# A graph network's one-hot aggregation: loops of five tiles for three, window ranges packed in one number, partial sums and keys moved to GpSimd

## Chip, cores and metric

The kernel runs on one core of a Trainium2 chip. The metric is the device time of one execution in microseconds. The engines are TensorE (PE, with its weight loads shown as PEld), VectorE (DVE), ScalarE (ACT), GpSimd (POOL) and SyncE (SP); each has a sequencer (shown as PEq or PEldq, DVEq and so on) that reads its own stream of instructions, register and branch instructions among them.

## The reference

The whole program is two layers of a network over 625 nodes with 512 features and 20000 edges sorted by `dst`. The change touches its first stage alone, which computes from the layer-normed features `xn`:

```python
hp = xn @ weight                                   # 625 x 512
msgs = hp[src] * edge_weight[:, None]
agg = relu(segment_sum(msgs, dst, num_segments=625))
```

and the counts of edges between each pair of nodes, which later attention layers use as a mask. `src` is uniform over the nodes; `dst` is `625 * u**2` for uniform u, sorted, so that low nodes have many edges. Behind it follow linear attention, a mixture of experts, two attention layers over the graph and a second mixture.

## The kernel before

**Tiles and windows.** The 20000 edges lie as 160 tiles (ET) of 125 edges, one edge on each partition. The nodes as destinations are cut into 20 windows (NW) of 32 (DW). For each window the kernel multiplies, over all tiles that hold an edge of it, a one-hot matrix of the edge's source (`one_src`, 125 edges x 628 columns) by a matrix of its destination (`hot_dst`, 125 x 128: the one-hot of the 32 destinations times the three bf16 parts of the weight, and once more by 1 for the count). Five matmuls of 128 columns, one for each 125 sources, make a tile. They add up in PSUM, in two banks a window, so that four windows have room.

**Start.** SyncE loads src, dst and the weights, then the features in one DMA, the product weights `gnnW` and `mixWq` beside it (lines 301 to 307). DVE works out windows, keys (1024 x window + source) and weight parts (lines 1111 to 1126), the first and the last tile of each window by PE's turning and two scans (1143 to 1151), the one-hot of the destinations for all tiles (`dst_one`, line 1139, ahead of the scans) and, behind the layer norm (1089 to 1105), its products with the three weight parts (1158, `dst_parts`). PE turns the numbers of the ranges into a row (543), DVE copies it to `bounds` (1153), PE turns the normalized rows (502) and multiplies them by gnnW (514, stage `hp`, 40 matmuls and as many weight loads), and ACT takes both out (913, 919). GpSimd zeroes two DRAM buffers by 35 DMAs (431, 434).

**The window loop.** PE and DVE run the same loops with k read at run time, three tiles (GT) a trip. DVE (line 1183) waits until PE has freed one of the GT buffers of `one_src`, then compares 628 numbers with `key - 1024 * w`, in one instruction of two operations. PE (line 581) waits for it and multiplies. Two matmuls by zero open a window's banks (569) and two close them (586). ACT copies the counts out (932); DVE adds the three weight parts (1170) one window later. Each window's first tile, its trips and the trips before it are three register loads from `bounds`, on PE (552 to 554) and on DVE (1162 to 1164). Both engines issue them one window ahead in program order, which puts them at the end of the window before. The loop's register steps are lines 575 and 1178.

**Behind it.** PE goes on with `mq` (526), whose banks wait for the sums, then turns the counts (599) and multiplies the summed weights by hp (605).

## Time and profile before

| | us |
|---|---|
| median of three runs | 1304.54 (1303.4 to 1308.75) |
| the profiled execution | 1310.6, its span 1309.1 |
| PE busy | 1117.8 (85%) |
| DVE busy | 540.6 (41%) |
| ACT busy | 347.6 (27%) |
| POOL busy | 83.4 (6%) |
| L581, PE, 975 matmuls | 85.6 busy, 44.5 idle before them |
| L1183, DVE, 195 comparisons | 66.9 busy, 63.3 idle before them |

A busy PE counts matmuls from start to modelled end, so neighbours overlap: 15 of 219 ns each may take 1.01 us in all. The stretches of the busy view give, for each engine, busy us and in brackets the number of instructions, in the order PE, PEld, DVE, ACT, POOL; then the clock granted to TensorE as a share of 2.4 GHz, the DMA engines' busy share, and GB/s. In the timeline the brackets at a row's end hold the idle time before it and what ended it; "issue" is nothing that the profile shows. Register instructions do not count as busy; the view by line and the chain of waits show them.

### The profile page before, as it was taken

To read this page: it belongs to the slowest core of one execution; us is meant where nothing else is said; L and a number is where in the kernel's file an instruction comes from. 1 tells how busy PE (TensorE), PEld (TensorE's weight loads), DVE (VectorE), ACT (ScalarE), POOL (GpSimd) and SP (SyncE) were. 2 spreads that over 40 slices of the span, in tenths; PEclk is the share of its full clock that TensorE was granted. 3 is DMA by queue.
4 is the path that set the end of the run, shared out by engine and by line. 5 is a ranking of instruction groups with operands and counts; after the bars stand their busy time and mean duration, and the time that the engine had idled before them with its cause. 6 is when DMAs were issued, how large, how long until landed. Compare 5 with 4: busy or idle time off the path is not lost.

```text
span 1309.1 us, 19993 instructions
## 1 busy us (share of the span) xinstructions
PE 1117.8 (85%) x7185; PEld 757.1 (58%) x7186; DVE 540.6 (41%) x1434; ACT 347.6 (27%) x881; POOL 83.4 (6%) x130
## 2 busy tenths in 40 slices
PE   2766679988999863999998659998979998988896
PEld 1456564465877651555554347777557777565652
DVE  7565565343555431111111035444325544376430
ACT  1000012012555430222222125554115555011320
POOL 5100000000000032001000050000000000000000
PEclk9897789998999975999999969999989999998898
DMA  7500004010100046940199671000111000000000
GB/s 198 141 1 1 1 1 193 32 57 17 31 26 3 1 185 244 388 177 19 60 401 398 244 271 43 25 9 2 64 73 41 25 9 2 33 1 0 1 1 39
DMA packets 18415, 113.06 MB, mean 86 GB/s; under 512 B 4718, under 2 KB 6245, under 8 KB 14135
## 3 DMA queue, kind: packets, MB, share of 16 engines
q1 hardware_dynamic: 12718, 100.95, 20.3%
q0 software_dynamic: 5632, 11.23, 3.3%
q8 instruction: 43, 0.70, 0.2%
q14 instruction: 22, 0.18, 0.0%
HBM read 103.04 MB, written 9.11 MB: 86 GB/s over the span
## 4 chain that ended last, share of the span: by engine, by line
PE 74%; DVE 8%; DMA 7%; issue 4%; ACT 3%; DVEq 3%; POOL 1%; SPq 0%; POOLq 0%; ACTq 0%
PE psum L514 11%; PE psum L669 8%; PE psum L819 7%; PE psum L800 7%; PE psum L692 5%; PE psum L526 5%; PE psum L723 5%; PE psum L674 4%; PE psum L705 4%; PE psum L581 4%; PE psum L878 3%; PE psum L900 3%; DMA arena<-in_moe_b 2%; PE psum L502 1%; DVE arena L1183 1%
## 5 line engine op out<-in xcount | busy, mean ns | idle before, releaser
L514 PE MATMUL psum<-arena 128*125 128x512 f32 x320 | 142.2, 605 | 2.6 <-ACT arena L913 2.0
L581 PE MATMUL psum<-arena 125*128 x975 | 85.6, 260 | 44.5 <-DVE arena L1183 41.4
L971 ACT ACTIVATE arena<-arena,small 125x625 f32<-125x625 f32 x120 | 97.0, 809 | 90.5 <-DVE small L1312 90.5
L669 PE MATMUL psum<-arena 128*128 128x313 f32 (+1 forms) x384 | 112.2, 443 | 8.5 <-DMA arena<-in_att 7.2
L800 PE MATMUL psum<-arena 128*64 128x512 f32 x448 | 101.7, 607 | 7.4 <-DMA arena<-in_moeW 6.0
L514 PEld LDWEIGHTS psum<-arena 128*125 128x125 f32 x320 | 60.9, 192 | 80.7 <-issue 74.9
L581 PEld LDWEIGHTS psum<-arena 125*128 125x128 bf16 x975 | 74.2, 119 | 54.5 <-issue 52.2
L819 PE MATMUL psum<-arena 128*64 128x256 f32 x896 | 99.8, 381 | 3.7 <-DMA arena<-in_moe_b 3.7
L1029 ACT ACTIVATE arena<-psum,cols 128x64 f32<-128x64 f32 x224 | 47.3, 361 | 198.6 <-PE psum L806 198.6
L669 PEld LDWEIGHTS psum<-arena 128*128 128x128 f32 x384 | 72.2, 194 | 37.9 <-issue 9.7
L1183 DVE TENSOR_SCALAR arena<-arena 125x628 bf16<-125x628 f16 x195 | 66.9, 382 | 63.3 <-issue 28.0
L1312 DVE CUSTOM_DVE_ANT_0 arena<-psum,cnt_adj 125x625 f32<-125x625 f32 x80 | 61.5, 807 | 71.8 <-PE psum L692 71.8
L723 PE MATMUL psum<-arena 125*64 125x125 f32 x1200 | 77.4, 274 | 9.5 <-ACT arena L983 9.0
L819 PEld LDWEIGHTS psum<-arena 128*64 128x64 f32 x896 | 63.4, 137 | 36.2 <-ACT arena L1029 5.8
L979 ACT ACTIVATE arena<-psum 125x500 f32<-125x500 f32 x120 | 63.7, 583 | 74.7 <-PE psum L705 74.7
L692 PE MATMUL psum<-arena 64*125 64x113 f32 x480 | 80.3, 453 | 0.0
L723 PEld LDWEIGHTS psum<-arena 125*64 125x64 f32 x1200 | 63.2, 136 | 25.1 <-ACT arena L983 12.3
L800 PEld LDWEIGHTS psum<-arena 128*64 128x64 f32 x448 | 32.6, 140 | 68.8 <-issue 66.8
L526 PE MATMUL psum<-arena 128*128 128x312 f32 (+1 forms) x256 | 68.3, 427 | 0.8 <-DVE arena L1332 0.8
L705 PE MATMUL psum<-ident,arena 125*125 125x125 f32 x480 | 67.8, 284 | 0.0
L692 PEld LDWEIGHTS psum<-arena 64*125 64x125 f32 x480 | 52.5, 183 | 24.9 <-issue 16.1
L502 PE MATMUL psum<-ident,arena 125*128 125x125 f32 x140 | 27.1, 366 | 44.4 <-DVE arena L1105 37.4
(242 smaller groups left out, 1335.6 us busy)
## 6 DMA issues: line engine op xcount, KB each, us to landing
arena<-in_moeW SPq DMA_DIRECT2D x16, 4096.0 KB, 17.7
arena<-in_att SPq DMA_DIRECT2D x36, 256.0 KB, 2.8
arena<-in_l1W SPq DMA_DIRECT2D x2, 2048.0 KB, 15.7
rows<-in_rows SPq DMA_DIRECT2D x1, 2500.0 KB
token_rows<-arena POOLq DMA_DIRECT2D x19, 128.0 KB, 10.5
expert_rows<-arena POOLq DMA_DIRECT2D x17, 128.0 KB, 10.0
arena<-token_rows POOLq DMA_DIRECT2D x16, 128.0 KB, 8.3
arena<-in_gnnWo SPq DMA_DIRECT2D x2, 1024.0 KB, 6.2
```

Of the source, the lines that this page charges most:

```text
L514: mm = pe.matmul(bank(b, NP, D), srcT[:, k, c * NP:(c + 1) * NP], ring[n % 2][:, k, :], start=(k == 0), stop=(k == KC - 1))
L526: mm = pe.matmul(bank(b, P, w), ring[n % 2][:, k, m * P:(m + 1) * P], srcT[:, k, o:o + w], start=(k == 0), stop=(k == KC - 1))
L581: mm = pe.matmul(psum[:, o + c * P:o + (c + 1) * P], one_src[:, s, c * NP:c * NP + P], hot_dst[:, bass.ds(e * P, P)], start=False, stop=False,
L669: mm = pe.matmul(bank(b, P, width), aw[:, w, k, :], srcT[:, k, o:o + width], start=(k == 0), stop=(k == KC - 1))
L692: mm = pe.matmul(psum[0:NP, at_:at_ + n], q[h * HD:(h + 1) * HD, c * NP:(c + 1) * NP], k[h * HD:(h + 1) * HD, o:o + n], start=True, stop=True)
L705: mm = pe.transpose(bank(3 + h, NP, NP, NP * j), Sx[u % 3][h][:, j * NP:(j + 1) * NP], ident[0:NP, 0:NP])
L723: mm = pe.matmul(psum[h * HD:(h + 1) * HD, 5 * 512 + 256:5 * 512 + 256 + NP], vv[i % 2][:, j, h * HD:(h + 1) * HD], PT[:, u % 2 * NC + j, ...
L800: mm = pe.matmul(psum[q * TT:(q + 1) * TT, 512 * b:512 * b + D], xsT[:, k4, :], EW1[par][:, k4, o:o + D], start=(k4 == 0), stop=(k4 == KC ...
L819: mm = pe.matmul(psum[q * TT:(q + 1) * TT, 4 * 512:4 * 512 + D // 2], hT[:, f, :], EW2[par][:, f, q * (D // 2):(q + 1) * (D // 2)], start= ...
L971: act.activation(Sx[u % 3][h], Sx[u % 3][h], ACT.Exp, bias=small[0:NP, 80 + n:81 + n], scale=-1.0, accum_out=small[0:NP, 120 + n:121 + n]) ...
L979: act.activation(PT[:, u % 2 * NC:u % 2 * NC + 4, h * NP:(h + 1) * NP], bank(3 + h, NP, 4 * NP).rearrange("p (j n) -> p j n", j=4), ACT.Co ...
L1183: ve.tensor_scalar(one_src[:, s, :], iota_src[:, 0:SW], float(1024 * w), key[:, bass.ds(e, 1)], ALU.add, ALU.is_equal).then_inc(hot_ready, 1)
```

## The change

- `GT` is 5 for 3: five buffers of `one_src`, five tiles a trip.
- `bounds` holds one number a window, 64 x first tile + trips. PE and DVE each read all twenty into registers ahead of the loops, take the parts by shift and mask (`tile_range`), and keep the sum of trips in a register. PE's reads stand behind hp.
- DVE compares in one operation, with keys that GpSimd has made for the window (`key_w`, two buffers, made a window ahead).
- ACT copies the counts and then the three weight parts of each window to SBUF (`parts`), GpSimd adds them by two instructions. PE's bank waits are for ACT's copy. The sums have to be there ahead of `agg`.
- The features come in five DMAs ahead of all product weights; gnnW is asked for once they are in, mixWq and the rest once gnnW is. GpSimd's zeroing waits for gnnW.
- `dst_one` moves from ahead of the range arithmetic to behind the layer norm; the statistics of each chunk of features move ahead of the copy of `bounds`.

```diff
@@ -26,11 +26,12 @@
...
 ET = EDGES // NP
-GT = 3
+GT = 5
+KG = -(-ET // GT)
 TP = ET + GT - 1
...
 NW = -(-N // DW)
-SW = N + GT
+SW = N + 3
 EX = 8
@@ -175,14 +176,17 @@
...
 zero_bf = take(NP, P, dt=BF16)
-zero_rows_sb = take(TT, D)
+zero_rows_sb = at(o_D + TP * 2 * DW, TT, D)
 t_lo, t_hi = take(ET // 2, 2), take(ET // 2, 2)
...
 w_end = take(NW, 8)
-w_cols = take(NW, 3)
+w_cols = take(NW, 2)
 n_i = take(NW, 2, dt=I32)
-bounds = take(1, 3, WMIN, dt=I32)
+bounds = take(1, WMIN, dt=I32)
+key_w = [take(NP, TP) for i in range(2)]
+parts = [at(o_T + 2 * KC * N + i * NC * 3 * DW, NP, NC, 3 * DW) for i in range(2)]
+assert o_D + TP * 2 * DW + D <= AR
 assert oa[0] <= o_cnt
@@ -238,7 +242,8 @@
...
 unit_full, freed_a, freed_v = sem("unit_full"), sem("freed_a"), sem("freed_v")
-ld_edges, ld_x, ld_const = sem("ld_edges"), sem("ld_x"), sem("ld_const")
+ld_edges, ld_const = sem("ld_edges"), sem("ld_const")
+ld_x = [sem(f"ld_x{c}") for c in range(NC)]
 ld_ring = [sem(f"ld_ring{i}") for i in range(2)]
...
@@ -296,16 +303,22 @@
...
+def tile_range(eng, packed):
+    return (eng.snap(packed >> 6, min_val=0, max_val=ET - 1), eng.snap(packed & 63, min_val=1, max_val=KG))
+
 @block.sync
...
     sp.dma_start(wgt, ins["edge_w"]).then_inc(ld_edges, 16)
-    sp.dma_start(xres[:], ins["x"]).then_inc(ld_x, 16)
+    for c in range(NC):
+        sp.dma_start(xres[:, c, :], ins["x"][:, c, :]).then_inc(ld_x[c], 16)
+    for c in range(NC):
+        sp.wait_ge(ld_x[c], 16)
     sp.dma_start(ring[0], ins["gnnW"]).then_inc(ld_ring[0], 16)
+    sp.wait_ge(ld_ring[0], 16)
     sp.dma_start(ring[1], ins["mixWq"]).then_inc(ld_ring[1], 16)
     sp.dma_start(cols[:], ins["cols"]).then_inc(ld_const, 16)
-    sp.wait_ge(ld_x, 16)
     sp.dma_start(rows[:], ins["rows"].partition_broadcast(NP)).then_inc(ld_const, 16)
@@ -424,7 +437,7 @@
...
-    pool.wait_ge(ld_x, 16)
+    pool.wait_ge(ld_ring[0], 16)
     pool.wait_ge(consts, 14)
@@ -433,7 +446,22 @@
...
-    pool.wait_ge(win_full, NW)
+    def window_keys(w):
+        pool.tensor_scalar(key_w[w % 2], key, float(-1024 * w), None, ALU.add).then_inc(keys_out, 1)
+
+    pool.wait_ge(key_ready, 1)
+    window_keys(0)
+    window_keys(1)
+    for w in range(NW):
+        pool.wait_ge(parts_out, w + 1)
+        if w + 2 < NW:
+            window_keys(w + 2)
+        n = min(DW, N - DW * w)
+        p3 = parts[w % 2].rearrange("p c (v d) -> p c v d", v=3)
+        pool.tensor_tensor(p3[:, :, 0, 0:n], p3[:, :, 0, 0:n], p3[:, :, 1, 0:n], ALU.add).then_inc(part_sum, 1)
+        pool.wait_ge(part_sum, w + 1)
+        pool.tensor_tensor(WT[:, :, DW * w:DW * w + n], p3[:, :, 0, 0:n], p3[:, :, 2, 0:n],
+                           ALU.add).then_inc(wt_out, 1)
     pool.memset(bd[:, :, :], 0.0).then_inc(bd_zero, 1)
@@ -539,19 +567,15 @@
...
     pe.wait_ge(range_cols, 1)
-    for v, spread in enumerate((ident, ident, upper)):
-        mm = pe.matmul(bank(5, 1, WMIN, WMIN * v), w_cols[:, min(v, 1):min(v, 1) + 1], spread[0:NW, 0:WMIN],
-                       start=True, stop=True)
-    mm.then_inc(range_rows, 1)
-    pe.wait_ge(range_ready, 1)
+    pe.matmul(bank(5, 1, WMIN), w_cols[:, 1:2], ident[0:NW, 0:WMIN],
+              start=True, stop=True).then_inc(range_rows, 1)
     rows_to_cols("xnT0", N1, lambda c: pe.wait_ge(ln_out, c + 1))
...
-    def tile_range(w):
-        return (pe.value_load(bounds[0:1, 0, w:w + 1], min_val=0, max_val=ET - 1),
-                pe.value_load(bounds[0:1, 1, w:w + 1], min_val=1, max_val=-(-ET // GT)),
-                pe.value_load(bounds[0:1, 2, w:w + 1], min_val=0, max_val=NW * -(-ET // GT)))
+    pe.wait_ge(range_ready, 1)
+    ranges = [pe.value_load(bounds[0:1, w:w + 1], min_val=1, max_val=64 * ET + KG) for w in range(NW)]
+    before = 0
@@ -559,19 +583,16 @@
...
     stage_out(pe, "hp")
-    ahead = tile_range(0)
     for w in range(NW):
-        first, k, before = ahead
+        first, k = tile_range(pe, ranges[w])
         o = window_banks(w)
         if w >= 4:
-            pe.wait_ge(wt_out, w - 3)
+            pe.wait_ge(parts_out, w - 3)
         for q in range(2):
...
             mm.then_inc(hot_free, GT)
-        if w + 1 < NW:
-            ahead = tile_range(w + 1)
         with pe.Fori(0, k) as j:
@@ -586,12 +607,14 @@
...
         mm.then_inc(win_full, 1)
+        before = pe.snap(before + k, min_val=w + 1, max_val=(w + 1) * KG)
...
         w = NW - 4 + (unit % 8) // 2
-        pe.wait_ge(wt_out, w + 1)
+        pe.wait_ge(parts_out, w + 1)
     product_cols("mq", T1, 1, window_out)
+    pe.wait_ge(cnt_out, NW)
     for c in range(NC):
@@ -599,6 +622,7 @@
...
         mm.then_inc(unit_full, 2)
+    pe.wait_ge(wt_out, NW)
     for c in range(NC):
@@ -929,9 +953,11 @@
...
         o, n = 512 * (2 * (w % 4)), min(DW, N - DW * w)
-        act.activation(cntT[:, :, DW * w:DW * w + n],
-                       psum[0:NP, o:o + NC * P].rearrange("p (c v d) -> p c v d", v=4, d=DW)[:, :, 3, 0:n],
-                       ACT.Copy).then_inc(cnt_out, 1)
+        sums = psum[0:NP, o:o + NC * P].rearrange("p (c x) -> p c x", x=P)
+        act.activation(cntT[:, :, DW * w:DW * w + n], sums[:, :, 3 * DW:3 * DW + n], ACT.Copy).then_inc(cnt_out, 1)
+        if w >= 2:
+            act.wait_ge(wt_out, w - 1)
+        act.activation(parts[w % 2], sums[:, :, 0:3 * DW], ACT.Copy).then_inc(parts_out, 1)
@@ -1119,7 +1145,7 @@
...
     ve.tensor_copy(w_part[:, 0, 0:ET], w_hi)
-    ve.scalar_tensor_tensor(key[:, 0:ET], win, 1024.0, srcf, ALU.mult, ALU.add)
+    ve.scalar_tensor_tensor(key[:, 0:ET], win, 1024.0, srcf, ALU.mult, ALU.add).then_inc(key_ready, 1)
     link(ve.tensor_tensor(w_rest, wgt, w_hi, ALU.subtract))
@@ -1136,8 +1162,6 @@
...
     i_.then_inc(range_in, 1)
-    ve.tensor_tensor(hot_dst4[:, :, 3, :], low.unsqueeze(2).to_broadcast([NP, TP, DW]),
-                     iota_dst.unsqueeze(1).to_broadcast([NP, TP, DW]), ALU.is_equal).then_inc(dst_one, 1)
     ve.wait_ge(range_turned, 1)
@@ -1148,43 +1172,36 @@
...
     link(ve.tensor_scalar(n_i[:, 1:2], n_i[:, 0:1], 16, None, ALU.logical_shift_right))
-    ve.tensor_copy(w_cols[:, 1:2], n_i[:, 1:2]).then_inc(range_cols, 1)
+    ve.scalar_tensor_tensor(w_cols[:, 1:2], w_cols[:, 0:1], 64.0, n_i[:, 1:2], ALU.mult,
+                            ALU.add).then_inc(range_cols, 1)
+    for c in range(NC):
+        ve.wait_ge(ld_x[c], 16)
+        i_ = chunk_stats(xres, c)
+    link(i_)
     ve.wait_ge(range_rows, 1)
-    ve.tensor_copy(bounds, bank(5, 1, 3 * WMIN).rearrange("p (v w) -> p v w", v=3)).then_inc(range_ready, 1)
-    ve.wait_ge(ld_x, 16)
-    layer_norm(0, xres, N1)
+    ve.tensor_copy(bounds, bank(5, 1, WMIN)).then_inc(range_ready, 1)
+    layer_norm(0, xres, N1, stats=False)
+    ve.tensor_tensor(hot_dst4[:, :, 3, :], low.unsqueeze(2).to_broadcast([NP, TP, DW]),
+                     iota_dst.unsqueeze(1).to_broadcast([NP, TP, DW]), ALU.is_equal).then_inc(dst_one, 1)
     ve.wait_ge(dst_one, 1)
...
-    def tile_range(w):
-        return (ve.value_load(bounds[0:1, 0, w:w + 1], min_val=0, max_val=ET - 1),
-                ve.value_load(bounds[0:1, 1, w:w + 1], min_val=1, max_val=-(-ET // GT)),
-                ve.value_load(bounds[0:1, 2, w:w + 1], min_val=0, max_val=NW * -(-ET // GT)))
-
-    def window_sums(w):
-        ve.wait_ge(cnt_out, w + 1)
-        o, n = 512 * (2 * (w % 4)), min(DW, N - DW * w)
-        parts = psum[0:NP, o:o + NC * P].rearrange("p (c v d) -> p c d v", v=4, d=DW)
-        ve.tensor_reduce(WT[:, :, DW * w:DW * w + n], parts[:, :, 0:n, 0:3], AX, ALU.add).then_inc(wt_out, 1)
-
     ve.wait_ge(range_ready, 1)
-    ahead = tile_range(0)
+    ranges = [ve.value_load(bounds[0:1, w:w + 1], min_val=1, max_val=64 * ET + KG) for w in range(NW)]
+    before = 0
     for w in range(NW):
-        first, k, before = ahead
-        if w + 1 < NW:
-            ahead = tile_range(w + 1)
+        first, k = tile_range(ve, ranges[w])
+        ve.wait_ge(keys_out, w + 1)
         with ve.Fori(0, k) as j:
...
                 ve.wait_ge(hot_free, (before + j) * GT + s + 1)
-                ve.tensor_scalar(one_src[:, s, :], iota_src[:, 0:SW], float(1024 * w), key[:, bass.ds(e, 1)],
-                                 ALU.add, ALU.is_equal).then_inc(hot_ready, 1)
-        if w:
-            window_sums(w - 1)
-    window_sums(NW - 1)
+                ve.tensor_scalar(one_src[:, s, :], iota_src[:, 0:SW], key_w[w % 2][:, bass.ds(e, 1)], None,
+                                 ALU.is_equal).then_inc(hot_ready, 1)
+        before = ve.snap(before + k, min_val=w + 1, max_val=(w + 1) * KG)
```

## Rows read from the trace of the kernel before

**Rows 1.** Busy time of each engine by stretch (columns: see the profile section).

```profile
53.40:60.00 6.60, 6.42 (x64) 6.04 (x65) 4.30 (x12) 0.00 (x0) 0.00 (x0) 0.57 0.25 55
60.00:90.00 30.00, 20.71 (x312) 17.10 (x308) 19.71 (x60) 0.64 (x3) 0.00 (x0) 1.00 0.01 2
90.00:183.50 93.50, 61.22 (x680) 55.35 (x681) 52.57 (x140) 5.17 (x17) 0.00 (x0) 0.73 0.00 1
```

**Rows 2.** Timeline, merged: start us, us, engine line operation, count, [idle before <-releaser].

```profile
61.10 1.05 PE L581 MATMUL psum<-arena 125*128 x15 [0.27 <-DVE arena L1183]
...
61.80 0.97 DVE L1183 TENSOR_SCALAR arena<-arena 125x628 bf16<-125x628 f16 x3 [0.35 <-PE psum L581]
...
100.12 4.35 PE L581 MATMUL psum<-arena 125*128 x42 [2.11 <-DVE arena L1183]
...
102.68 1.35 DVE L1183 TENSOR_SCALAR arena<-arena 125x628 bf16<-125x628 f16 x3 [0.25 <-PE psum L581]
```

**Rows 3.** Chain of waits at a boundary between windows: start us, us, what.

```profile
124.74 0.31 DVEq L1163
...
125.37 0.30 DVEq L1164
```

**Rows 4.** PE's queue by line: count, ns min/median/max, first to last start us.

```profile
L552 PEldq TENSOR_LOAD <-arena x2: 522/614/707, 47.5 to 50.4; - x2
...
L552 PEldq TENSOR_LOAD <-arena x18: 297/302/310, 71.2 to 177.5; - x18
...
L552 PEldq FUSED_REGOPS  x18: 168/168/168, 71.6 to 177.8; - x18
...
L581 PEldq FUSED_REGOPS  x3: 69/69/153, 73.6 to 74.1; - x3
...
L575 PEldq ALU_OP  x1: 32/32/32, 74.3 to 74.3; - x1
...
L575 PEldq FUSED_REGOPS  x1: 56/56/56, 74.7 to 74.7; - x1
```

**Rows 5.** Timeline, the last window's first matmuls.

```profile
182.64 1.01 PE L581 MATMUL psum<-arena 125*128 x15 [0.31 <-DVE arena L1183]
```

**Rows 6.** Timeline of the start, 14 to 51 us.

```profile
14.81 0.30 DVE L1143 TENSOR_TENSOR arena<-psum,arena 20x160 f32<-20x160 f32 x1
...
17.24 0.14 DVE L1151 CAST arena<-arena 20x1 f32<-20x1 int32 x1
...
19.29 3.07 DVE L1089 BATCH_NORM_STATS2 small<-xres 125x6 f32<-125x512 f32 x5 [0.68 <-DMA xres<-in_x]
...
26.16 16.48 DVE L1158 TENSOR_TENSOR arena<-arena 125x5184 bf16<-125x5184 bf16 x3
...
29.29 17.43 PE L514 MATMUL psum<-arena 128*125 128x512 f32 x40 [0.68 <-ACT arena L913]
...
46.76 0.60 ACT L919 ACTIVATE arena<-psum 125x512 f32<-125x512 f32 x1 [2.84 <-PE psum L514]
...
50.34 0.28 PE L569 MATMUL psum<-arena 125*128 125x64 f16 x2 [3.62 <-issue]
```

**Rows 7.** By line, the expert stage: PE's queue behind 32 matmuls, and these.

```profile
L804 PEldq FUSED_REGOPS  x1: 43/43/43, 567.0 to 567.0; - x1
...
L800 PE MATMUL psum<-arena x32: 592/592/592, 564.4 to 570.9; 128*64 128x512 f32 x32
```

**Rows 8.** DMA issues: what, count, KB each, us to landing.

```profile
arena<-in_mixWp SPq DMA_DIRECT2D x1, 1024.0 KB, 4.9
```

**Rows 9.** By line and in groups: GpSimd operations, and DVE's beside one.

```profile
L442 POOL TENSOR_TENSOR arena<-arena,rows x5: 1257/1260/1648, 470.0 to 475.2; 125x512 f32<-125x512 f32 x5
...
L1105 DVE TENSOR_SCALAR arena<-arena,small x5: 545/546/551, 468.1 to 469.9; 125x512 f32<-125x512 f32 x5
...
L413 POOL IOTA arena<- 20x160 f32 x1 | 0.3, 254 | 0.0
```

**Rows 10.** Groups by shape, DVE at 200 to 206 us: busy us, mean ns.

```profile
L1205 DVE TENSOR_SCALAR cnt_adj<-psum 125x625 f32<-125x625 f32 x2 | 1.6, 800 | 0.0
```

More of the change, by code:

```diff
@@ L252, in build @@
         hot_ready, hot_free = sem("hot_ready"), sem("hot_free")
-        win_full, wt_out, cnt_out = sem("win_full"), sem("wt_out"), sem("cnt_out")
+        win_full, cnt_out = sem("win_full"), sem("cnt_out")
+        key_ready, keys_out = sem("key_ready"), sem("keys_out")
+        parts_out, part_sum, wt_out = sem("parts_out"), sem("part_sum"), sem("wt_out")
         fm_min, fm_exp = sem("fm_min"), sem("fm_exp")
```

## Prediction

> **What bounds it now.** I read the busy time by stretch first. The whole aggregation stage, in which one-hot matrices are built by VectorE and multiplied by TensorE, lies between 53.4 and 183.5 us, 130.1 of the span's 1309.1, and in it no engine is full: look at how PE and DVE both stay near two thirds or below, and at the granted clock, 0.57 and then 1.00 in the first stretches and 0.73, a mix of 1.2 and 2.4 GHz, over the last 93.5 us [rows 1]. Then the timeline inside the stage. At full clock a trip of three tiles repeats every 1.33 us: PE works 1.05 and waits 0.27 for DVE, DVE works 0.97 and waits 0.35 for PE [rows 2]. Neither is slow; with three buffers the round trip through both sets the pace. At 1.2 GHz the trip takes 1.60 (DVE's 1.35 and 0.25 of waiting for PE) and PE goes through without a gap, 42 matmuls in 4.35: there it is PE's own pace, 0.53 a tile [rows 2]. Third, the chain between two windows: DVE's queue spends 0.63 us on each of three register loads (the second begins at 124.74, the third at 125.37), and PE stands idle 2.11 us at such a boundary [rows 2, 3]. PE's own queue has the same loads, 0.30 for the read and 0.15 to 0.17 for the check behind it, about 0.66 each, so it would be no earlier [rows 4]. The one boundary where no load is left costs PE 0.31 us of idle time instead [rows 5]. Fourth, the start: DVE is busy with the one-hot parts until 42.6, PE with hp until 46.7 and ACT until 47.4, then three loads on PE to 50.3, and three more until its first product at 53.4 [rows 1, 6].
>
> Everything behind 183.5 waits for this stage by the chain, and no load with a fixed time falls due there, so what the stage saves moves the end by as much.
>
> **How many tiles.** Counting the reference's inputs, the 20 windows touch 37, 16, 13, 11, 9, 9, 8, 8, 7, 7, 6, 6, 6, 6, 6, 5, 6, 5, 5 and 3 tiles. In threes that is 65 trips and 195 tiles; the trace has 975 = 5 x 195 matmuls there. In fives it is 46 trips (8, 4, 3, 3, then eleven times 2, 1, 2, 1, 1, 1) and 230 tiles: 35 tiles more are multiplied, each 0.28 to 0.30 at full clock (15 matmuls in 1.01 to 1.05 us, 219 ns the last) and 0.53 at half [rows 2, 5].
>
> **Loops of five.** Five buffers lift the round trip: 1.33 us for five tiles would be 0.27 a tile, below what either engine needs. What is left is PE's queue. Its waits for the three tiles start from 73.6 to 74.1, the loop's add and register step, with the branch between them, run at 74.3 and 74.7, and with the next wait's own 0.1 a trip of three can't be under about 1.2 [rows 4]. Two more tiles at 0.24 to 0.28 make 1.7 to 1.8; I take 1.71. DVE starts a comparison every 0.29 (three in 0.97, the last 0.38), so 1.45 a trip and about 1.55 with its branch: just faster [rows 2]. 46 trips x 1.71 = 78.7. In the first 6 us after PE's idle time the clock is 1.2 GHz as it is now [rows 1], where a trip takes 5 x 0.53 = 2.67: two trips more by 0.96, +2.
>
> **Packed ranges.** Twenty times three loads leave both queues' windows. Instead each window has three register steps (shift, mask, running sum). The trace has one of this kind a trip, 56 ns [rows 4], 0.1 with its gap; at most it costs what follows a load, 0.36. I take 0.1, since the loop's own step has bounds too and no check stands behind it: 0.3 a window, 0.3 to 1.1. With the boundary's 0.07 above a trip's own end (from the one boundary without loads [rows 5]) 20 x 0.37 = 7. Sum of the stage: 78.7 + 2 + 7 = 88.
>
> **The loads move to the front, twenty in a row, on each queue.** On DVE they run under the one-hot parts (0.63 x 20 = 12.6 in 22 us) as its first six do now. On PE they stand behind hp. 20 x 0.66 = 13.2, or 17.6 at the 0.88 that the 0.52 to 0.71 us reads of 47 to 54 us gave [rows 4]. How far can PE's queue run ahead of the matmuls? In the expert stage the register step behind 32 matmuls ran at 567.0 while they went on to 570.9, with 18 of the 32 still ahead [rows 7]. Eighteen of hp's 40 at 0.43 (17.43 us for 40 [rows 6]) are 7.7 us.
>
> **The start itself.** dst_one (5.5 us) leaves the gap before the range arithmetic, which so begins 4.7 us earlier, at 10.1 behind PE's turning, and ends at 12.7 instead of 17.4 [rows 6]. The features come alone now: 1.25 MB at the pace of 1 MB in 4.9 us [rows 8] is 6.1 us, with the five issues at 10 to 11 us, so the statistics start at 12.7 and not 19.3, and hp's weights, asked for after them, land near 16 to 17 (bound 22, where they would be used). 6.6 us earlier, less 0.3 for the bounds' copy that now stands behind them: the normalized rows and all of hp move by -6.3, hp from 29.3 to 23.0 and its end from 46.7 to 40.4, ACT's to 41.1 [rows 6]. DVE's four one-hot operations (5248 elements for 5184) run 19.9 to 42.2, as late as now: this edit buys nothing on DVE, 6.3 us on PE. PE's loads then run from 40.4 - 7.7 = 32.7 to 46 or 50; I take 47.4, and with it the opening matmul. From there to the first product lie one comparison and two handovers, which in a trip take 0.35 and 0.62 (61.10 to 61.80 to the next product at 62.43), with 0.2 for the register steps 1.2: 48.6 instead of 53.4, -4.8. Bounds 44.4 (all of them under hp) and 59.6 (none).
> The Trainium skill (Advanced Engine Details and Errata, Engine Queue Depths) gives TensorE's queue as 64 entries; then 64 of hp's 80 loads and matmuls would be queued, PE's registers would be ready by 40 to 44, and DVE's 42.2 would decide: 4 us better. The row above shows no more than 36 entries.
>
> **Sums elsewhere.** DVE loses 20 reductions of 0.65; ACT copies 480 columns (about 0.58, like its 512-column copies of 0.60 [rows 6]) beside 0.31 for the counts: 0.9 a window of at least 2.1, hidden. PE's bank wait goes to the copy, four windows back: nothing. The last sum is needed behind mq, 17 us later: nothing. GpSimd gets a key step and two additions a window. Additions of 512 columns take 1.26, so 160 at most 0.55 each, 160 numbers by one input near an iota's 0.25 and up to 0.35 [rows 9]: 1.45 a window, 29 in all. Keys are made a window ahead: hidden, unless GpSimd falls behind. It might: one of its additions at 470.0 began beside the last two of DVE's five normalizing operations (to 470.5) and took 1.65 for 1.26 [rows 9], so GpSimd waits while such a DVE operation runs. DVE is free for 88 - 230 x 0.29 = 21 us of 88; GpSimd wants 29. Between 0 and 19 (below); I take 5. Keys 0 and 1 stand behind its 35 zeroing DMAs, which started when the features were in, at 19.3, and now start when hp's weights are, near 17: through before the loops as now; were they late, the first product would be so one for one. **The single comparison**: same size and types, one operation less. No row separates the two, so 0, from -0.1 a comparison (hidden behind PE's queue anyway) to the case below.
>
> **Sum.** Stage 93 for 130.1: -37. Start -4.8. Together -42. The profiled execution took 1310.6 with its launch, so 1268.6 in its terms; the median of the runs shown is 6.1 lower, 1304.5, so **1262.5**.
>
> **Rivals.**
> - *PE's twenty loads don't hide.* Against: the run-ahead in [rows 7]. For: they are twice as many as it covers. First product at 59.6, stage as forecast: 1304.5 + 6.2 - 37 = 1274. Chance 0.12.
> - *The clock stays a mix.* Now it falls in the short windows and not in the long ones [rows 1]; PE will be busier in each (a boundary of 0.7 us for 2.1 idle), which speaks against it. If half of the 28 trips from window 4 on are at 1.2 GHz: 14 x 0.96 = +13.4, 1276; all of them 1289. Chance 0.15.
> - *GpSimd and DVE exclude each other.* Each of GpSimd's 1.45 us then also stops DVE: 46 x 1.55 + 20 x 0.33 + 29 = 107 for the stage, 1304.5 - 4.8 - 23 = 1277. DVE's operations beside the slow addition took 551 for 545 ns, so it was GpSimd alone that paid; but they were first. The Trainium skill (SBUF — State Buffer, SBUF: two separate sides) has this as a rule: an exclusive lock for a whole instruction, against a DVE operation in a two-port mode. Chance 0.14.
> - *Slower: the comparison in its new form loses its rate.* The two-operation form does 628 columns in 0.38; other comparisons of DVE take 0.80 for 625 [rows 10]. At 0.72 from start to start 230 of them are 165 us, the stage 172: 1304.5 - 4.8 + 42 = 1342. It decides from about 0.55 a comparison on, where 230 of them equal the time now. Speaking against it: types, sizes and memory are unchanged. Chance 0.05. With it goes a remainder of 0.04 for a start or a register step that costs far more than any row.
> - *The change does little*, since the boundary is waits and not loads: against it stands the one boundary without loads. 1300 to 1306, 0.04.
>
> **Range and chances.** Forecast 0.46 (1250 to 1272). Unknown terms: start -9 to +6, register steps 0 to +16, GpSimd -5 to +14, clock 0 to +27. From 1247 (all at their good ends: start 44.4, stage 86, less a little) to 1292 lie the forecast and the first three rivals. About 0.5%, 6.5 us, is what a measurement can tell from no change: faster by more 0.88, within 0.05, slower 0.07.
>
> **What would show it.** Right: COMPARE_BRANCH of PE's loop 46 times; trips 1.7 apart at full clock with PE idle 0.3 in each; PE idle 0.6 to 0.8 between windows; first product near 48.6 and last near 142; clock 1.00 behind 60 us; DVE comparisons at 0.38. Wrong: TENSOR_LOADs on PE ending behind 52; PE trips of 2.67; DVE comparisons ended by GpSimd's key step, or GpSimd additions above 1 us; checks behind each register step. The forecast fails if PE's queue needs over 2.2 us a trip, or if the clock is at 1.2 GHz for most of the stage.

## Result and the profile after

The changed kernel takes 1322.2 us (median of 4 runs, 1319.0 to 1325.9) where the kernel before took 1304.0 on the same chip: ratio 1.0133, interval 1.0095 to 1.0171. It is 1.3% slower, with an interval clear of 1, where 1262.5 us was forecast, and outside the range.

| | before | after | forecast |
|---|---|---|---|
| profiled execution, us | 1310.6 | 1319.0 | 1268.6 |
| first product of a trip, us | 53.4 | 48.1 | 48.6 |
| last product's start | 183.4 | 199.4 | about 142 |
| stage of windows, us | 130.0 | 151.3 | 93 |
| behind the last product, to the span's end | 1125.7 | 1117.8 | as before |

The start came 5.3 us earlier, as forecast. The stage became 21 us longer instead of 37 shorter. What lies behind it holds the same work; in the profiles of the changed kernel and of the twelve kernels below it took 1118 to 1126 us, so a difference of some us between single profiles can come from there. Stage and first product are each read from one profile too.

Groups of the page (busy us, mean ns of one | idle time before, its releaser): PE's products, their weight loads, VectorE's comparisons.

```profile
L602 PE MATMUL psum<-arena 125*128 x1150 | 86.3, 242 | 63.5 <-issue 43.1
...
L602 PEld LDWEIGHTS psum<-arena 125*128 125x128 bf16 x1150 | 78.5, 110 | 69.7 <-issue 69.6
L1202 DVE TENSOR_SCALAR arena<-arena 125x628 bf16<-125x628 f16 x230 | 77.1, 393 | 75.6 <-PE psum L602 67.0
```

PE stands idle 63.5 us ahead of these products, and 43.1 of it wait for nothing the profile shows ("issue"). DVE's 75.6 us of idle time wait for PE. The comparisons themselves cost 393 ns: nothing wrong there.

Busy time of each engine by stretch of the stage, columns as in [rows 1]:

```profile
48.10:64.00 15.90, 14.76 (x204) 13.87 (x204) 13.30 (x42) 0.00 (x0) 0.00 (x0) 0.83 0.31 75
64.00:100.00 36.00, 23.78 (x396) 21.98 (x395) 25.74 (x75) 4.59 (x12) 9.92 (x18) 1.00 0.00 1
100.00:140.00 40.00, 18.39 (x291) 16.98 (x289) 17.54 (x56) 3.83 (x10) 8.36 (x16) 0.94 0.00 1
140.00:199.80 59.80, 32.25 (x347) 30.31 (x346) 19.84 (x59) 6.12 (x16) 12.69 (x23) 0.64 0.01 2
```

PE's busy share falls from stretch to stretch: 14.76 of 15.90 us, then 23.78 of 36, 18.39 of 40. (In the last stretch it rises to 32.25 of 59.8, because at the lower clock each product takes longer.) The granted clock is a mix of 1.2 and 2.4 GHz in the first stretch (0.83), at its upper level of 2.4 GHz to 100 us, just below (0.94) to 140, and a mix again (0.64) over the last 60 us. So this is not a stage with a bad engine but one that gets worse as it goes. The timeline shows how, first in window 0:

```profile
56.99 1.56 PE L602 MATMUL psum<-arena 125*128 x25 [0.32 <-DVE arena L1202]
...
58.77 1.57 PE L602 MATMUL psum<-arena 125*128 x25 [0.22 <-DVE arena L1202]
59.50 1.56 DVE L1202 TENSOR_SCALAR arena<-arena 125x628 bf16<-125x628 f16 x5 [0.22 <-PE psum L602]
...
60.56 0.56 PE L602 MATMUL psum<-arena 125*128 x7 [0.23 <-DVE arena L1202]
```

From 56.99 to 58.77 a trip of five tiles takes 1.78 us, with PE idle 0.22 to 0.32 for DVE: the trip that was forecast at 1.71. In window 9 the same two rows read:

```profile
118.84 1.56 PE L602 MATMUL psum<-arena 125*128 x25 [1.94 <-issue]
...
119.60 1.56 DVE L1202 TENSOR_SCALAR arena<-arena 125x628 bf16<-125x628 f16 x5 [2.05 <-PE psum L602]
...
122.66 1.05 PE L602 MATMUL psum<-arena 125*128 x16 [2.26 <-issue]
123.41 0.38 DVE L1202 TENSOR_SCALAR arena<-arena 125x628 bf16<-125x628 f16 x1 [2.26 <-PE psum L602]
```

Here a trip takes 3.82 us (118.84 to 122.66). The products still need 1.56, but PE is idle 2.26 ahead of the next trip, and DVE idles just as long behind it. PE's queue in that gap (count, ns min/median/max, first to last start):

```profile
L600 PEldq ALU_OP  x16: 32/39/43, 120.5 to 122.1; - x16
L600 PEldq FUSED_REGOPS  x1: 56/56/56, 122.2 to 122.2; - x1
```

Line 600 is the wait for a tile's comparison. Its value needs `before`, and ahead of one wait PE's queue works through sixteen ALU_OPs, of 0.04 us each and 0.107 from one to the next (120.5 to 122.1 for 16). Over the whole stage, for PE's wait and for DVE's:

```profile
L600 PEldq ALU_OP  x748: 32/36/43, 48.1 to 197.6; - x187
L600 PEldq FUSED_REGOPS  x38: 50/56/56, 64.0 to 196.5; - x38
```
```profile
L1201 DVEq ALU_OP  x745: 40/45/53, 48.2 to 194.0; - x187
L1201 DVEq FUSED_REGOPS  x38: 63/70/77, 62.8 to 192.9; - x38
```

On PE, 184 of them are what the five waits of 46 trips need (one for each tile but the first); the other 564 are the running sum. `before = pe.snap(before + k)` doesn't put a number into a register. `before` stays an expression over the packed ranges of all earlier windows, (r0 & 63) + (r1 & 63) + ..., and it is worked out anew wherever it is used, which is in every trip. Counting a mask and an addition for each earlier window, the 46 trips hold 318 such pairs, 636 steps; the trace has 564 ALU_OPs and one FUSED_REGOPS in each of the 38 trips behind window 0, which must stand for the rest.

So a trip grows by 0.2 us with every window, from 1.78 us to 5.2 and more near the end (from 180.40 to 185.59, with the matmuls by zero that close and open a window in between):

```profile
180.40 2.82 PE L602 MATMUL psum<-arena 125*128 x25 [2.24 <-issue]
...
185.59 2.15 PE L602 MATMUL psum<-arena 125*128 x25 [2.24 <-issue]
```

The products of the trip at 180.40 run at the lower clock, 2.82 us instead of 1.56, and still PE is idle for 2.24 before the next ones: even there it is the queue that sets the trip, not the clock. Two trips of window 12 show it side by side: the one from 142.58 us has its products at 1.2 GHz (2.82 us) and takes 4.51 us, the one from 147.09 has them at 2.4 GHz (1.56 us) and takes 4.43. And it is PE's queue more than DVE's, which works out the same sums: the chain of waits from 100 to 199 us is PE's products for 46.0%, "issue" right ahead of them for 37.7%, DVE's comparisons for 12.4% and DVE's queue for some 4%. No run left the expression on one of the two queues alone.

### The profile page after: what moved, and what is told of

The parts are those of the page before. It is cut to its first block, busy times and chain, and to the rows that moved or that the text cites. A ratio compares the mean times of both kernels' runs of the same rounds, so it can differ in the third digit from the quotient of the medians.

```text
span 1317.2 us, 21595 instructions
## 1 busy us (share of the span) xinstructions
PE 1113.8 (85%) x7356; PEld 755.5 (57%) x7357; DVE 541.5 (41%) x1449; ACT 356.9 (27%) x901; POOL 119.0 (9%) x190
## 4 chain that ended last, share of the span: by engine, by line
PE 75%; DVE 8%; issue 6%; DMA 5%; ACT 3%; DVEq 1%; POOL 1%; SPq 0%; POOLq 0%; ACTq 0%
PE psum L542 9%; PE psum L693 9%; PE psum L843 7%; PE psum L824 6%; PE psum L602 6%; PE psum L716 5%; PE psum L554 5%; PE psum L747 5%; PE psum L698 4%; PE psum L729 4%; PE psum L902 3%; PE psum L924 3%; DMA arena<-in_moe_b 2%; PE psum L629 2%; DVE arena L1202 2%
## 5 line engine op out<-in xcount | busy, mean ns | idle before, releaser
L602 PE MATMUL psum<-arena 125*128 x1150 | 86.3, 242 | 63.5 <-issue 43.1
L602 PEld LDWEIGHTS psum<-arena 125*128 125x128 bf16 x1150 | 78.5, 110 | 69.7 <-issue 69.6
L1202 DVE TENSOR_SCALAR arena<-arena 125x628 bf16<-125x628 f16 x230 | 77.1, 393 | 75.6 <-PE psum L602 67.0
```

The lines of the kernel that those rows point to most:

```text
L602: mm = pe.matmul(psum[:, o + c * P:o + (c + 1) * P], one_src[:, s, c * NP:c * NP + P], hot_dst[:, bass.ds(e * P, P)], start=False, stop=False,
L1202: ve.tensor_scalar(one_src[:, s, :], iota_src[:, 0:SW], key_w[w % 2][:, bass.ds(e, 1)], None, ALU.is_equal).then_inc(hot_ready, 1)
```

## Experiments

Times are medians; ratios are to the kernel before, measured beside each (1306 to 1307 us), and go by all runs, so they need not be the quotient of the medians. First product and stage come from each kernel's one trace. The start is the same in eight of the kernels (total, total3, hoist, two_op, one_input, both, sums_dve, fours), but for GpSimd's first keys, and yet their first products came at 47.9 to 52.0 us: that much single profiles differ there.

| kernel | us | ratio, 95% interval | first product | stage |
|---|---|---|---|---|
| total | 1271.1 | 0.9731 (0.9675, 0.9786) | 48.9 | 97.1 |
| total3 | 1278.2 | 0.9780 (0.9722, 0.9839) | 50.8 | 106.7 |
| lazy_before | 1295.5 | 0.9896 (0.9859, 0.9934) | 53.7 | 120.1 |
| lazy_mask | 1368.1 | 1.0463 (1.0418, 1.0508) | 53.7 | 192.1 |
| start_only | 1301.0 | 0.9957 (0.9936, 0.9977) | 47.4 | 128.8 |
| hoist | 1267.1 | 0.9683 (0.9646, 0.9719) | 51.5 | 93.8 |
| two_op | 1265.9 | 0.9687 (0.9654, 0.9721) | 52.0 | 92.4 |
| one_input | 1271.9 | 0.9737 (0.9704, 0.9771) | 51.2 | 93.0 |
| both | 1264.7 | 0.9670 (0.9648, 0.9691) | 51.9 | 87.3 |
| sums_dve | 1263.2 | 0.9670 (0.9641, 0.9699) | 51.0 | 85.9 |
| fours | 1260.0 | 0.9666 (0.9633, 0.9699) | 47.9 | 90.8 |
| loads_spread | 1262.1 | 0.9666 (0.9647, 0.9684) | 43.2 | 97.6 |

### Is it the expression?

**total** keeps the changed kernel and holds the sum in one register of each queue; the same on DVE's side:

```
-            before = 0
+            total = pe.alloc_register("total_pe")
+            pe.reg_mov(total, 0)
             ...
+                before = pe.snap(total, min_val=w, max_val=w * KG)
             ...
-                before = pe.snap(before + k, min_val=w + 1, max_val=(w + 1) * KG)
+                pe.reg_add(total, total, k)
```

> The changed kernel, with one difference: the running number of trips lives in a register of its own on PE and on DVE, set to 0, read at each window's start, and increased by k once at each window's end, where the changed kernel wrote the sum as an expression that is worked out again in every trip (in the trip at 118.8 us 14 extra ALU_OPs on PE, 2 for each earlier window, about 0.1 us each). Theory (the expression is what fails the prediction): no ALU_OPs that grow with the window, trips of about 1.8 us in all windows at full clock, first product still near 48, last near 140 to 148, so 52 to 60 us less than the changed kernel: 1262 to 1272 us. Rival (GpSimd's key step and additions on the port it shares with DVE): trips still grow or DVE's comparisons still wait, the stage keeps 130 us or more, over 1300 us. Rival (TensorE's clock): the stage is at 1.2 GHz from about 140 us on as it was, 1280 to 1290.

Measured 1271.1 us, 51 less than the changed kernel. PE's waits have no ALU_OP left but a tile's own, and behind 64 us the clock stays at its upper level (PE's wait line, then the stretches):

```profile
L602 PEldq ALU_OP  x184: 32/32/42, 48.9 to 145.2; - x184
```
```profile
48.80:64.00 15.20, 14.02 (x194) 13.21 (x195) 12.68 (x40) 0.00 (x0) 0.00 (x0) 0.83 0.29 73
64.00:100.00 36.00, 29.68 (x463) 26.00 (x460) 30.34 (x87) 5.36 (x14) 11.25 (x21) 1.00 0.00 1
100.00:146.00 46.00, 37.77 (x574) 32.49 (x573) 38.11 (x104) 9.19 (x24) 20.93 (x36) 1.00 0.01 2
```

564 ALU_OPs fewer make the stage 54.2 us shorter, 0.096 us for each, where they lay 0.103 apart on average (0.107 in the gap above): nine tenths of their time had been on the path. And the lower clock of the last 60 us is gone with PE's waiting.

**lazy_before** puts such an expression alone into the kernel before: its third number a window is no longer loaded but summed from the loaded counts.

```
-                        pe.value_load(bounds[0:1, 2, w:w + 1], ...)
+                before = pe.snap(before + k, min_val=w + 1, ...)
```

> The kernel before, with one difference: the third number of each window (trips before it) is not loaded but written as the sum of the trips of all earlier windows, as the changed kernel does. Here each earlier window is one addition (its trips are a loaded register), not a mask and an addition. Theory: each trip of window w gets w more ALU_OPs of about 0.1 us on PE and 0.07 to 0.08 on DVE, 416 in all by the trips (13, 6, 5, 4, six times 3, nine times 2, 1): 42 us of PE's queue, of which one load a window saved (0.66 x 19 = 12.5) and some slack in the trips at 1.2 GHz go off: slower than before by 10 to 30 us. Rival (the expression costs nothing that matters): one load less a window, faster by up to 12 us.

A miss: it got 11 us faster. The trace tells why. The loop's own register line, with up to nineteen terms in it, and the wait's line:

```profile
L575 PEldq FUSED_REGOPS  x65: 50/175/195, 53.4 to 171.8; - x65
L575 PEldq ALU_OP  x65: 32/32/32, 54.2 to 173.5; - x65
```
```profile
L579 PEldq ALU_OP  x140: 32/32/42, 53.7 to 173.2; - x140
L579 PEldq FUSED_REGOPS  x28: 42/128/180, 119.1 to 172.3; - x28
```

A sum of plain registers is put together into one FUSED_REGOPS, 175 ns where [rows 4] shows 56, once a trip, and the wait's line has 140 ALU_OPs in all. In exchange one load of three is gone from each window, and the stage is 9.9 us shorter. So "an expression instead of a loaded value" was not yet the cause; my second guess was that the mask in it is.

**lazy_mask** is lazy_before with `& 63` on each loaded count, which changes no value.

```
-                        pe.value_load(bounds[0:1, 1, w:w + 1], ...)
+                        pe.snap(pe.value_load(bounds[0:1, 1, w:w + 1], ...) & 63, ...)
```

> The kernel before with the sum of earlier trips as an expression (as in lazy_before, 1295.5 us), and each loaded count masked with 63 ahead of the sum, which changes no value. Theory (the mask is what costs: two ALU_OPs for each earlier window in every trip, 0.205 us together in the changed kernel's trace, while a plain addition is folded into the FUSED_REGOPS): 65 trips hold 416 such pairs, 85 us of PE's queue, of which some 20 us hide beside the products: 1360 us, 1335 to 1380. Rival (the length of the sum costs, or the one load less, whatever is summed): as lazy_before, 1290 to 1300.

```profile
L580 PEldq ALU_OP  x864: 32/36/43, 53.7 to 244.6; - x173
L580 PEldq FUSED_REGOPS  x52: 50/56/56, 72.9 to 244.0; - x52
```
```profile
100.00:245.00 145.00, 67.78 (x625) 60.03 (x624) 49.03 (x129) 4.89 (x16) 0.00 (x0) 0.52 0.00 1
```

1368.1 us: 724 ALU_OPs more than lazy_before's 140, a stage 72.0 us longer, 0.099 us for each. It is the same price as between the changed kernel and total, from the other side, and here too the clock falls to a mix (0.52) as PE waits more. The mask keeps the terms from being put together, and the sum then costs about two ALU_OPs a term in every trip (724 for 416 terms). The only difference between the two kernels is the mask on the loaded count, so this settles the cause.

**hoist** is total with `first` and `k`, too, written into registers once a window, three register steps a window as the prediction had them:

```
-            return (eng.snap(packed >> 6, ...), eng.snap(packed & 63, ...))
+            eng.reg_alu(first_r, packed, 6, ALU.logical_shift_right)
+            eng.reg_alu(k_r, packed, 63, ALU.bitwise_and)
+            return (eng.snap(first_r, ...), eng.snap(k_r, ...))
```

> The kernel total (1271.1 us), with first and k also written into registers once a window, so that no shift and no mask is left inside a trip. Theory (PE's queue is part of what sets a trip's length): two ALU_OPs of 0.09 us with their gaps leave each of 46 trips, 0 to 5 us of the time: 1269, 1266 to 1272. Rival (the comparisons of DVE set the trip, at 0.29 us a tile and 0.6 us beside GpSimd): nothing, 1271 within 1.5.

1267.1 us, with a stage of 93.8 us for the 93 of the forecast. Against total the times' intervals overlap; the stage is 3.3 us shorter, within the expected 0 to 5.

### What are the other parts worth?

**start_only** is the kernel before with only the reordered start (chunks of the features ahead of hp's weights, statistics ahead of the one-hot, dst_one behind them).

> The kernel before with the reordered start alone: features in five DMAs ahead of the weights, gnnW behind them, statistics of the chunks ahead of the copy of the bounds, the one-hot of the destinations behind the layer norm, zeroing behind gnnW. Loops, loads, sums and keys as before. Theory: first product of the windows moves from 53.4 to about 48.2 (DVE's one-hot parts end near 42.2, then six loads on PE), everything behind it shifts: 1299 us, 5 less. Rival (the start is hidden by other work or the later transfers fall into the loop): 1304.

1301.0 us, 5 less; as expected. The stage is 128.8 us, as good as before's 130.0.

**total3** is total with `GT = 3`, so 65 trips and 195 tiles.

> As the run with the total in a register, but three tiles a trip and three buffers instead of five (65 trips, 195 tiles). It tells what the fives are worth without the expression. Theory: trips of 1.33 us bound by the round trip through three buffers, boundaries of about 1 us: 65 x 1.33 + 20 x 0.4 = 94 at full clock, some of it at 1.2 GHz (1.60): a stage of 95 to 105, 1270 to 1282 us. If fives are worth much, it is 10 or more above the run with five; if the 35 extra tiles eat the gain, the same within 5.

Fives against threes: a stage of 97.1 for 106.7 us, 7 us in the medians, though the intervals of the two ratios overlap. The expectation had "10 or more" or "within 5" and got neither. Total3 against start_only, which has threes too, tells what the packed ranges are worth, with the sums and keys on GpSimd: a stage of 106.7 for 128.8 us and 1278.2 for 1301.0. That is the largest gain in the change, 22 us of the stage. Part of it comes back by the clock: the granted clock over the stage is 0.78 in start_only and 0.99 in total3. **fours** is the kernel "both" (below) with `GT = 4`: 54 trips, 216 tiles.

> The kernel both with loops of four tiles instead of five: 54 trips and 216 tiles instead of 46 and 230. Theory (14 tiles fewer at 0.31 to 0.37 us, and 8 ends of a trip more at 0.35 to 0.5 us): 1 us less, within 3: 1261 to 1267. Rival (a shorter buffer starves PE: the wait for DVE's first comparison grows with it): 1270 or more, as threes cost 7 us.

1260.0 us is 1 below the expected range. There is no difference to fives in the times (0.9666 and 0.9670), with a stage of 90.8 us for 87.3: the trips added cost the stage 3.5 us more than the tiles saved give, and the times can't tell it.

**two_op** is total with DVE's comparison of before and no key by GpSimd.

```
-                        ve.tensor_scalar(one_src[...], iota_src[...], key_w[w % 2][:, bass.ds(e, 1)], None, ALU.is_equal)
+                        ve.tensor_scalar(one_src[...], iota_src[...], float(1024 * w), key[:, bass.ds(e, 1)], ALU.add, ALU.is_equal)
```

> The kernel total with DVE's comparison of before (add and is_equal from the one key) and without GpSimd's 20 key operations. Theory (both comparisons run at the same rate, 0.382 us in the trace of before and 0.376 in total's; GpSimd's key is free): 1271 within 2. Rival (the single comparison is worth what its place in the change suggests): 1276 or more.

The comparison in both forms (total's with one operation, two_op's with two):

```profile
L1206 DVE TENSOR_SCALAR arena<-arena x230: 369/377/717, 48.2 to 144.9; 125x628 bf16<-125x628 f16 x115
```
```profile
L1197 DVE TENSOR_SCALAR arena<-arena x230: 370/378/680, 51.3 to 143.0; 125x628 bf16<-125x628 f16 x115
```

377 and 378 ns in the median, 382 on average in the kernel before. The single comparison buys nothing, and its keys cost GpSimd 0.64 us a window. The time without them, 1265.9 us, is lower by 5 and outside both expectations, though the intervals of the ratios overlap; the stage is 4.7 us shorter.

**both** joins hoist and two_op.

> The kernel two_op (1265.9 us: a real total, DVE's comparison with two operations, no keys by GpSimd) with first and k written into registers once a window, as in hoist. Theory (a trip waits for DVE's comparisons, so PE's two ALU_OPs matter little once the total is a register; the 3 us between hoist and total were mostly this): the stage of windows 91 to 92 us, 1264, 1260 to 1268. Rival (both savings add up, 4 and 5 us): 1259.

The stage is 87.3 us where the theory had 91 to 92, so the two savings add up there (93.8 and 92.4 from 97.1), as the rival had it; the time, 1264.7, is near the theory's 1264 and can't tell.

**one_input** is total with GpSimd's two additions turned into operations of one input, so it leaves the middle and the low part of the weights out of the sums.

> The kernel total, with GpSimd's two additions a window turned into two operations with one input each (a constant 0 is added); so the middle and the low part of the weights are left out of the sums. In total's trace 38 comparisons of DVE that lie beside L461 or L463 took 0.63 to 0.72 us and 172 with nothing of GpSimd's or its one-input key operation beside them 0.376 to 0.39. Theory (it is the two inputs that collide): the comparisons all take 0.38, 10 us of DVE's time go, and 5 to 10 of them from the time: 1264, 1260 to 1267. Rival (anything that GpSimd does in that place collides): the long comparisons stay, 1268 to 1272. Second rival (DVE's excess is hidden beside PE): the long comparisons go and the time stays at 1271 within 2.

```profile
L1206 DVE TENSOR_SCALAR arena<-arena x230: 365/384/480, 50.5 to 143.4; 125x628 bf16<-125x628 f16 x115
```
```profile
L461 POOL TENSOR_SCALAR arena<-arena 125x160 f32<-125x160 f32 x19 | 13.3, 702 | 0.5
L463 POOL TENSOR_SCALAR arena<-arena 125x160 f32<-125x160 f32 x19 | 12.9, 678 | 1.6
```
```profile
L461 POOL TENSOR_TENSOR arena<-arena 125x160 f32<-125x160 f32 x19 | 10.7, 561 | 0.6 <-ACT arena L962 0.2
L463 POOL TENSOR_TENSOR arena<-arena 125x160 f32<-125x160 f32 x19 | 10.4, 550 | 1.5
```

No theory in full. The comparisons' worst case goes from 717 to 480 ns, but most of those beside the two operations still take 0.42 to 0.48 us, and GpSimd's operations now take 0.69 us on average where the additions had 0.55. Part of that is their form: the four of full size that overlap DVE least take 0.60 to 0.61, as the additions take 0.52 with nothing beside them. So comparisons are still hindered, less each and more of them, and the time stayed.

**sums_dve** is both with a window's sums again by one reduction of DVE, with no copy by ACT and no addition by GpSimd.

> The kernel both with the sums of a window as before: one reduction of DVE from PSUM (1.35 us in the trace of before) instead of ACT's copy and GpSimd's two additions. Theory (DVE sets the trips, so 20 reductions cost 1.1 us each, less the 10 us of DVE's time that its comparisons lose beside GpSimd's additions): 12 us more, 1276, 1269 to 1284. Rival (the reduction hides beside PE's five tiles, and the long comparisons go): 1256 to 1263.

```profile
L1200 DVE TENSOR_SCALAR arena<-arena x230: 374/379/387, 50.4 to 135.5; 125x628 bf16<-125x628 f16 x115
```
```profile
L1200 DVE TENSOR_SCALAR arena<-arena 125x628 bf16<-125x628 f16 x230 | 71.9, 379 | 13.2 <-PE psum L585 8.5 <-PE psum L595 2.8 <-issue 0.2
L1185 DVE TENSOR_REDUCE arena<-psum 125x160 f32<-125x480 f32 (+1 forms) x20 | 12.8, 640 | 1.0 <-ACT arena L950 1.0
```
```profile
L1204 DVE TENSOR_SCALAR arena<-arena 125x628 bf16<-125x628 f16 x230 | 77.6, 403 | 18.1 <-PE psum L592 8.6 <-PE psum L602 7.5 <-issue 0.3
```

The rival held. (The reduction that the theory put at 1.35 us takes 0.65 in the trace of before, line 1170, as the prediction had it.) With GpSimd idle no comparison takes over 387 ns (379 on average, 403 in both), and the reductions, 12.8 us, fit in beside the time in which DVE waits for PE's buffers. The stage is 85.9 for 87.3, the ratio the same to the fourth digit. Moving the sums brought nothing.

**loads_spread** is both with only three of PE's twenty loads ahead of the first window, and one in each of the first seventeen windows for the third window after it.

```
-            ranges = [pe.value_load(...) for w in range(NW)]
+            ranges = [packed_range(w) for w in range(3)]
             ...
+                if w + 3 < NW:
+                    ranges.append(packed_range(w + 3))
```

> The kernel both, with PE's 20 loads of packed ranges cut to three ahead of the first window and one in each window for the third window after it. Theory (PE's 20 loads end last ahead of the first window: 50.4 us in two_op against 43.4 for ACT's last copy of hp, 46.7 and 41.3 in the changed kernel): first product at 44 to 45 us instead of 48 to 52, a load of 0.3 to 0.6 us more in a window's queue, which mostly hides: 1260, 1256 to 1264. Rival (a load in a window is paid in full, 17 x 0.65 us = 11): 1268 or more.

The chain ahead of the first product, of both and of loads_spread, and the loads in the stage:

```profile
42.98 0.61 ACT arena L943
43.59 7.30 issue
50.89 0.30 PE psum L592 x2
...
51.91 0.29 PE psum L602
```
```profile
36.34 5.43 DVE arena L1193
41.77 0.39 issue
42.16 0.30 PE psum L595 x2
...
43.19 7.91 PE psum L607 x90
```
```profile
L575 PEldq TENSOR_LOAD <-arena x16: 297/300/503, 58.3 to 130.4; - x16
L575 PEldq FUSED_REGOPS  x16: 167/173/173, 58.9 to 130.7; - x16
L575 PEldq SEQ_ASSERT  x16: 18/18/18, 59.1 to 131.0; - x16
```

The first product comes 8.7 us earlier, right behind DVE's one-hot parts, and the stage is 10.3 us longer. One of the seventeen loads lies ahead of the first product; 10.3 us over the sixteen behind it are 0.64 us for each, paid in full as the rival had it, but the time is the theory's and the same as both's. Loads ahead of the stage and loads inside cost alike here, as far as intervals of 2 to 3 us can tell. Of the 8.7 us some 4 may be the spread of profiles: in fours, with the same start as both, the first product came at 47.9.

## Why the prediction was wrong, step by step

**What bounds it now: held.** The stage is where both the gain and the loss lie. That boundaries are paid by register work on the queues held as well (total3 against start_only, 22 us), in a way I did not carry far enough.

**Packed ranges: the step that failed.** I wrote "each window has three register steps (shift, mask, running sum)", 0.1 us each, "0.3 a window, 0.3 to 1.1". The price of one step was right: 0.096 to 0.103 us. Their number was not. I counted them where they stand in the text, once a window; they run where their value is used, once a trip, and the running sum has two for every earlier window. Hoist, which does have three a window, has the forecast's stage, 93.8 us for 93, and a ratio of 0.9683 where 1262.5 / 1304.5 is 0.968. So the term was forecast at 6 us, and as the change wrote it it cost 57.5 more than with the three steps (151.3 - 93.8). A row of before could have told me: in [rows 4] the FUSED_REGOPS on line 581 runs three times in one trip, once a tile. I read them as the waits; they stand on the product's line, and the only value of that line that is worked out at run time is the tile's place in `hot_dst`. So such values are made at the use. In the kernel before `before` was a loaded register, and a wait's value took one short instruction or none; the diff turns it into a sum that grows.

**Loops of five: right.** 1.71 us forecast for a trip, 1.78 in window 0, and the first two, at 1.2 GHz, 2.63 and 2.67 where I had 2.67. By the starts of every 25th product, from window 4 on, the median trip inside a window takes 1.71 us in hoist and in both. One that crosses into the next window takes 2.38 in hoist, 0.67 more, and 2.12 in both, 0.41 more, where I had 0.37. Both has no keys by GpSimd, so the boundary was sized right and the rest in hoist comes with the keys. Its whole stage is 87.3 us, where the sum had 88 ahead of the 5 for GpSimd. The sign I named for failure, "PE's queue needs over 2.2 us a trip", came true, but no rival carried it: the range's upper end took register steps at +16 us, once a window, and only a remainder of 0.04 was left for a register step "that costs far more than any row". The step cost what the rows say; there were more of them. My rival on the slower side was the comparison's rate, and that didn't move (two_op).

**The start: right**, with its parts. Forecast and measured: hp from 23.0 and 23.2 to 40.4 and 40.6 us, ACT's last copy 41.1 and 41.3, one-hot parts 42.2 and 42.15, PE's last load 47.4 and 46.7, first product 48.6 and 48.1. The statistics of the features began at 12.7 and 12.46. Hp's weights landed at 20.5 us, later than the 16 to 17 I had, but below the bound of 22 where they are used. The rival that the loads don't hide was half true: where all twenty stand ahead of the stage they ended at 46.3 (fours) to 50.4 us (two_op), and the first product came at 47.9 to 52.0. Without most of them it came at 43.2, 1.2 us before the bound of 44.4 that I had for loads all hidden. But loads_spread shows that they cost the same inside the stage.

**The clock: a result, not a rival.** It fell as I feared, to 0.64, but with PE's waiting: it stays at 1.00 behind 64 us in the kernel total, with 1150 of the same products and PE idle 16.3 us ahead of them instead of 63.5.

**GpSimd and DVE: the size was near, the payer wrong.** I took 5 us with GpSimd as the one that waits. In the kernel total it is mostly DVE: its comparisons average 422 ns against 379 in sums_dve, so 230 x 0.043 = 9.9 us, 5.5 in both; the additions take 0.55 for 0.52 with nothing beside them. What reaches the stage comes with the keys: it is 4.7 us shorter without them in two_op than in total and 6.5 in both than in hoist. Without the additions it is only 1.4 shorter (sums_dve against both, where DVE has the reductions to do instead). Whether the keys cost it by the shared place or by DVE's wait for them, no run separates. Ahead of the stage it was GpSimd that paid:

```profile
39.52 3.82 POOL L450 TENSOR_SCALAR arena<-arena 125x164 f32<-125x164 f32 x2
```

two keys of 0.63 took 3.82 us beside DVE's products of two inputs. The Trainium skill (SBUF — State Buffer, SBUF: two separate sides) says that whichever of a GpSimd operation and a DVE operation of certain kinds starts first holds the shared ports for its whole instruction and the other waits. Both directions above fit it. Whether the sizes do is not shown: in one_input, comparisons beside an operation of GpSimd of 0.66 us took 0.42 to 0.48 us for 0.38, which is less than a wait for a whole instruction would often give, and no row here tells which comparisons are of those kinds.

**Sums elsewhere and the single comparison: right at nothing.** I gave 0 for both; sums_dve is as fast as its partner and two_op no slower. What the change gains it gains by the start (5 us), by one register load a window for three (some 22 us, total3 against start_only; by their number and not their place, as loads_spread has it), and by fives (7 in the medians).

## What to carry to other kernels

A named value in a program for a queue's registers may be an expression and not a number. Ask of every such value where it is used, how often, and how many terms it has by then; a running sum or an unpacked field that a loop uses belongs in a real register, written once outside of the loop. With that one edit this change goes from 1.3% slower to 2.7% faster, and with first and k in registers too and the comparison left alone to 3.3% (both); the parts that moved work to other engines could all have been left out.

## What the runs showed of the hardware

- An ALU_OP takes 0.03 to 0.04 us on PE's queue and 0.103 from one to the next on average in the changed kernel (0.04 to 0.05 and 0.078 on DVE's). 564 of them (total) and 724 (lazy_mask) were hardly hidden: 0.096 and 0.099 us of the stage for each.
- Additions of registers are put together into one FUSED_REGOPS (175 ns in the median, 195 at most, with up to nineteen terms, for 56 with one; lazy_before); terms with a mask are not (lazy_mask, the changed kernel).
- A register load on PE inside the stage costs it 0.64 us (loads_spread: 0.30 for the read, 0.17 and 0.02 for the bounds, the rest gaps). Ahead of the stage single reads took up to 0.9 us; in both it was the last four, begun behind 45 us. What slowed them no run shows: from 30 to 40 us, with the DMA engines busy 0.96 and 0.98 of the time, reads took 0.30.
- PE's compare-and-branch at a trip's end took 0.07 to 0.08 us in the last trip of each window, where the loop ends, and 0.207 to 0.251 in each trip that goes back to the loop's start, in every kernel here. The Trainium skill (Advanced Engine Details and Errata, Control Flow Timing) gives about 0.108, which no row here shows.
